# Output projection by pairs of expert chunks for both token tiles of a half batch

## The reference

```python
rw = _gating(hidden_states, sim_matrix, gates)
q = jnp.einsum('bte,bted->btd', rw, jnp.einsum('btc,ecd->bted', hidden_states, q_proj))
...
attn = jnp.einsum('bqk,bkd->bqd', jax.nn.softmax(scores, axis=-1), v)
mixed = attn[:, :, None, :] * rw[..., None]
return jnp.einsum('bted,edc->btc', mixed, o_proj)
```

## Time and profile before

| What | Value |
|---|---|
| time, median of 3 runs | 992.86 us (987.39 to 992.89) |
| the profiled execution | 990.36 us, span 988.6 us |
| mean granted TensorE clock | 0.959 |
| TensorE busy | 924.0 us, 93% of the span |
| VectorE busy | 619.8 us, 63% |
| ScalarE busy | 232.6 us, 24% |
| GpSimd busy | 173.7 us, 18% |
| transfers | 53.68 MB, 54 GB/s over the span |

### The profile page before, as it was taken

One profiled execution on the slowest core, in us unless ns is written; L12 is line 12 of the kernel. 1 busy time (PEld: TensorE's weight loads), 2 busy tenths in 40 slices (PEclk: granted clock), 3 DMA queues, 4 the chain that ended last, 5 costly groups with the idle time before them and its releaser, 6 DMA issues.

```text
span 988.6 us, 15673 instructions
## 1 busy us (share of the span) xinstructions
PE 924.0 (93%) x5000; PEld 844.8 (85%) x5000; DVE 619.8 (63%) x1747; ACT 232.6 (24%) x543; POOL 173.7 (18%) x344
## 2 busy tenths in 40 slices
PE   4787866999999999999999999999999999999987
PEld 3455544999999999998999999999999999999976
DVE  7788773666565656565656575747574657565743
ACT  6666651121111111111111121111111111111111
POOL 4554443530101110101010010101010101001100
PEclk9788886999999999999999999999999999999997
DMA  5454623110202020101010101010101010100010
GB/s 177 150 184 161 213 87 117 65 54 2 64 1 65 1 64 1 65 1 55 10 55 9 54 11 53 11 54 11 53 11 54 11 48 16 48 17 29 26 40 24
DMA packets 30574, 53.68 MB, mean 54 GB/s; under 512 B 7241, under 2 KB 7241, under 8 KB 30386
## 3 DMA queue, kind: packets, MB, share of 16 engines
...
...
## 4 chain that ended last, share of the span: by engine, by line
PE 77%; DVE 4%; issue 2%; DVEq 0%; ACT 0%; POOL 0%; POOLq 0%
PE psQ L1254 51%; PE psO L1341 17%; PE psM L1327 2%; PE psT L1293 2%; PE psT L1229 1%; PE psT L1265 1%; PE psT L1274 1%; PE psQ L1341 1%; DVE acc L1114 1%; PE psM L1311 1%; DVE resid L1144 0%; PE psM L1308 0%; PE psT L1282 0%; DVE neg_mx L1148 0%; DVE b_stats L1059 0%
## 5 line engine op out<-in xcount | busy, mean ns | idle before, releaser
L1254 PE MATMUL psQ<-Wqkv_hi,hT_hi 128*128 128x384 f32 (+1 forms) x1024 | 352.9, 345 | 1.4 <-DVE hT_lo L1055 1.4
L1254 PE MATMUL psQ<-Wqkv_lo,hT_hi 128*128 128x384 f32 (+1 forms) x1024 | 347.3, 339 | 0.0
L1254 PE MATMUL psQ<-Wqkv_hi,hT_lo 128*128 128x384 f32 (+1 forms) x1024 | 347.1, 339 | 0.0
L1114 DVE SCALAR_TENSOR_TENSOR acc<-psQ,RW,acc 128x192 f32<-128x192 f32 x448 | 165.6, 412 | 235.2 <-PE psQ L1254 234.0
L1254 PEld LDWEIGHTS psQ<-Wqkv_hi,hT_hi 128*128 128x128 f32 x1024 | 193.3, 189 | 3.6 <-DVE hT_lo L1055 1.8
L1254 PEld LDWEIGHTS psQ<-Wqkv_lo,hT_hi 128*128 128x128 f32 x1024 | 193.2, 189 | 2.1
L1254 PEld LDWEIGHTS psQ<-Wqkv_hi,hT_lo 128*128 128x128 f32 x1024 | 192.8, 188 | 0.0
L891 POOL TENSOR_TENSOR pow_tmp<-b_mv,eps 128x1 f32<-128x1 f32 x32 | 6.1, 190 | 560.9 <-DVE b_mv L1061 560.8
L1341 PE MATMUL psO<-Wo_hi,mixedT_hi 128*128 128x512 f32 x248 | 98.8, 398 | 0.0
L1341 PE MATMUL psO<-Wo_lo,mixedT_hi 128*128 128x512 f32 x248 | 97.5, 393 | 0.0
L1341 PE MATMUL psO<-Wo_hi,mixedT_lo 128*128 128x512 f32 x248 | 97.4, 393 | 0.0
...
## 6 DMA issues: line engine op xcount, KB each, us to landing
...
```

What stands on the lines that cost most here:

```text
L1114: dve.scalar_tensor_tensor(out=acc[e][:], in0=src, scalar=w, in1=acc[e][:], op0=ALU.mult, op1=ALU.add).then_inc(expert_added, 1)
L1254: last = pe.matmul(psQ[g % 4][:, 0:first_col(g) + PW], x[:, c * P:(c + 1) * P], w[:, c, E + g * PW - first_col(g):E + (g + 1) * PW], start ...
```

## The change

Mixes stay in order, but the second half's mixes are issued one slot later (8 to 11, not 7 to 10), and each mix is followed two slots later by its own part of the projection: two chunks for both tiles of the half, 6 matmuls into `psO` for the even tile and 6 into `psM`, the bank of the scores, for the odd tile. So a half's projection stands in four equal pieces of 12 matmuls, in slots 25 to 28 and 10 to 13; before, it stood in slots 27, 28 and 30 (12, 12 and 24 matmuls) and 11, 12 and 14. The residual additions move from slots 29, 31, 13 and 15 to 28, 29, 13 and 14. Since `psM` is in use until the odd tile's residual addition, the scores of the third tile go from slot 29 to 30 and wait for `y_ready`, and every step behind them in slots 29 to 7 moves one slot on as well: gates, transposes of the probabilities (now slots 0 and 5), q and k of the fourth tile (slot 1), its scores (slot 3), the gates' transposes (6) and the values (7). The semaphore `projected` is replaced by `mix_used` (one step per piece) and `even_projected` (the even tile is complete). SyncE's issues keep their order. The number of instructions that compute is the same on each engine.

```diff
--- before.py
+++ after.py
@@ -34,18 +34,17 @@
 
 
 LEAD = 16
-QK_T_AT = {12: 0, 16: 1, 28: 2, 0: 3}
-SCORES_AT = {16: 0, 18: 1, 29: 2, 2: 3}
-GATES_AT = {17: 0, 19: 1, 30: 2, 3: 3}
-PROBS_T_AT = {18: 0, 20: 1, 31: 2, 4: 3}
-GATES_T_AT = {21: 0, 5: 1}
-VALUES_AT = {22: 0, 6: 1}
+QK_T_AT = {12: 0, 16: 1, 28: 2, 1: 3}
+SCORES_AT = {16: 0, 18: 1, 30: 2, 3: 3}
+GATES_AT = {17: 0, 19: 1, 31: 2, 4: 3}
+PROBS_T_AT = {18: 0, 20: 1, 0: 2, 5: 3}
+GATES_T_AT = {21: 0, 6: 1}
+VALUES_AT = {22: 0, 7: 1}
 MIX_AT = {23: (0, 0), 24: (0, 1), 25: (0, 2), 26: (0, 3),
-          7: (1, 0), 8: (1, 1), 9: (1, 2), 10: (1, 3)}
+          8: (1, 0), 9: (1, 1), 10: (1, 2), 11: (1, 3)}
 MIX_LO_AT = {k + 1: job for k, job in MIX_AT.items()}
-PROJECT_AT = {27: [(0, 0)], 28: [(0, 1)], 30: [(1, 0), (1, 1)],
-              11: [(2, 0)], 12: [(2, 1)], 14: [(3, 0), (3, 1)]}
-Y_AT = {29: 0, 31: 1, 13: 2, 15: 3}
+PROJECT_AT = {k + 2: job for k, job in MIX_AT.items()}
+Y_AT = {28: 0, 29: 1, 13: 2, 14: 3}
 STATS_SLOT, NORM_SLOT, H_T_SLOT = 1, 3, 5
 GATES_1_SLOT, GATES_3_SLOT = 0, 1
 ADD_AT = {0: (), 1: (0, 1), 2: (2,), 3: (3,), 4: (4,), 5: (5,), 6: (6,), 7: (7,)}
@@ -773,7 +772,7 @@
     mix_hi, mix_lo = sem("mix_hi"), sem("mix_lo")
     spread_made = sem("spread_made")
     gatesT_zero = sem("gatesT_zero")
-    projected = sem("projected")
+    mix_used, even_projected = sem("mix_used"), sem("even_projected")
     y_ready = sem("y_ready")
     gate_in_ready, gate_exp_ready = sem("gate_in_ready"), sem("gate_exp_ready")
     rw_ready = sem("rw_ready")
@@ -810,7 +809,7 @@
 
     def tile_copies(k, qkv, lead):
 
-        if k in QK_T_AT and (lead if k == 0 else qkv):
+        if k in QK_T_AT and (lead if k < 2 else qkv):
             return QK_T_AT[k]
         return None
 
@@ -822,10 +821,6 @@
 
         blocks = 2 * (i - i % 2) + 3
         return half[:].rearrange("p (s l) -> p s l", l=P)[:, 1 - i % 2:blocks:2, :]
-
-    def y_bank(i, qkv):
-
-        return psO if qkv or i < TILES - 1 else psQ[0]
 
     def v_twice(i):
 
@@ -857,26 +852,24 @@
                 sp.dma_start(resid[i % 2][:], row(x2_dram, b, i)).then_inc(res_in[i % 2], 16)
 
             def body(b, qkv, lead, prep):
-                for j in range(TILES):
-                    if qkv and (prep or j < TILES - 1):
+                for k in range(SLOTS):
+                    j, g = divmod(k, PAIRS)
+                    if g == 0 and qkv and (prep or j < TILES - 1):
                         sp.wait_ge(h_ready, TILES * b + j + 1)
                         sp.dma_start(X2[:], row(x2_dram, b, j + 1)).then_inc(x2_in, 16)
-                    if not lead and j < 2:
+                    if not lead and g == 0 and j < 2:
                         for n in range(OC // 2):
                             load_wo(j * OC // 2 + n)
-
-                    if lead and j == 0:
+                    if lead and k == 2:
                         load_resid(b - 1, 2)
                         load_resid(b - 1, 3)
-                    if lead and j == 1:
-                        store_y(b - 1, 2)
-                        store_y(b - 1, 3)
-                    if qkv and j == 2:
+                    if lead and k in (14, 15):
+                        store_y(b - 1, k - 12)
+                    if qkv and k == 18:
                         load_resid(b, 0)
                         load_resid(b, 1)
-                    if qkv and j == 3:
-                        store_y(b, 0)
-                        store_y(b, 1)
+                    if qkv and k in (29, 30):
+                        store_y(b, k - 29)
 
             bodies(sp, body, [])
             for p in range(2):
...
@@ -1014,10 +1007,9 @@
                         h, u = MIX_AT[k]
                         act.wait_ge(moved_lo, moves.step())
 
-                        if h == 1:
-                            act.wait_ge(projected, 8 * ab + 3 + u // 2)
-                        elif not isinstance(ab, int) or ab >= 1:
-                            act.wait_ge(projected, 8 * (ab - 1) + 7 + u // 2)
+                        h2 = 2 * ab + h
+                        if not isinstance(h2, int) or h2 >= 1:
+                            act.wait_ge(mix_used, 4 * h2 + u - 3)
                         act.activation(mixedT[0][:, 2 * u:2 * u + 2, :], mixed_f[u % 2][:], ACT.Copy
                                        ).then_inc(mix_hi, 1)
                     if attn and k in SCORES_AT:
@@ -1138,10 +1130,13 @@
 
                     if attn and k in Y_AT:
                         i = Y_AT[k]
-                        a = TILES * ab + i
-                        dve.wait_ge(projected, 2 * a + 2)
-                        dve.wait_ge(res_in[i % 2], 16 * (2 * ab + i // 2 + 1))
-                        dve.tensor_tensor(resid[i % 2][:], y_bank(i, qkv)[:], resid[i % 2][:], ALU.add).then_inc(y_ready, 1)
+                        h2 = 2 * ab + i // 2
+                        if i % 2 == 0:
+                            dve.wait_ge(even_projected, h2 + 1)
+                        else:
+                            dve.wait_ge(mix_used, 4 * h2 + 4)
+                        dve.wait_ge(res_in[i % 2], 16 * (h2 + 1))
+                        dve.tensor_tensor(resid[i % 2][:], (psO, psM)[i % 2][:], resid[i % 2][:], ALU.add).then_inc(y_ready, 1)
                     if attn and k in SCORES_AT:
                         i = SCORES_AT[k]
                         dve.wait_ge(scored, TILES * ab + i + 1)
...
@@ -1298,10 +1293,8 @@
 
                         if i % 2 == 1:
                             pe.wait_ge(exp_done, TILES * ab + i)
-                        elif i == 2:
-                            pe.wait_ge(attT_out, 2 * ab + 1)
-                        elif not isinstance(ab, int) or ab >= 1:
-                            pe.wait_ge(attT_out, 2 * ab)
+                        elif i == 2 or not (isinstance(ab, int) and ab == 0):
+                            pe.wait_ge(y_ready, TILES * ab + i)
                         pe.wait_ge(moved_lo, qk_moved[i])
                         cols = slice(0, (i + 1) * P)
                         q = qkT[:, 0, i * P:(i + 1) * P]
@@ -1328,19 +1321,23 @@
                                              x[:, s * 2 * P:s * 2 * P + cols.stop],
                                              start=(m == 0), stop=(m == len(order) - 1), skip_group_check=True)
                         last.then_inc(valued, 1)
-                    for i, part in PROJECT_AT.get(k, []) if attn else []:
-                        a = TILES * ab + i
-                        bank = y_bank(i, qkv)
-                        if part == 0 and bank is psO and not (isinstance(ab, int) and a == 0):
-                            pe.wait_ge(y_ready, a)
-                        pe.wait_ge(wo_lo, OC)
-                        for c in range(part * HALF, (part + 1) * HALF):
-                            if c % 2 == 0:
-                                pe.wait_ge(mix_lo, 8 * ab + 4 * (i // 2) + c // 2 + 1)
-                            for n, (x, w) in enumerate(products(mixedT, Wo)):
-                                last = pe.matmul(bank[:], x[:, c, place(i)], w[:, c, :],
-                                                 start=(c == 0 and n == 0), stop=(c == OC - 1 and n == 2))
-                        last.then_inc(projected, 1)
+                    if attn and k in PROJECT_AT:
+                        h, u = PROJECT_AT[k]
+                        h2 = 2 * ab + h
+                        if u == 0:
+                            pe.wait_ge(wo_lo, OC)
+                            pe.wait_ge(attT_out, h2 + 1)
+                            if not (isinstance(h2, int) and h2 == 0):
+                                pe.wait_ge(y_ready, 2 * h2 - 1)
+                        pe.wait_ge(mix_lo, 4 * h2 + u + 1)
+                        for i in range(2):
+                            for c in range(2 * u, 2 * u + 2):
+                                for n, (x, w) in enumerate(products(mixedT, Wo)):
+                                    last = pe.matmul((psO, psM)[i][:], x[:, c, place(i)], w[:, c, :],
+                                                     start=(c == 0 and n == 0), stop=(c == OC - 1 and n == 2))
+                            if u == 3 and i == 0:
+                                last.then_inc(even_projected, 1)
+                        last.then_inc(mix_used, 1)
                 if qkv:
                     since_h[0] = moves.k - h_count
```

6 lines of the change are left out of this document (3 added, 3 removed).

## The result

The changed kernel takes 1006.56 us (median of 4 runs, 1004.00 to 1007.29), the kernel before in the same session 992.00 (4 runs, 987.39 to 992.89). The ratio is 1.0156, with a 95% interval of 1.0127 to 1.0186: slower by about 15 us. So the two profiles, 13.6 us apart, can be compared term by term.

A forecast was written before the change was run, and what follows sets the result against it. TensorE's matmuls were taken to bound the kernel, so only its waits could change the time. 990.4 - 4.9 + 14.2 - 0.4 = 999.3 us, plus 5.1 for the clock, gave 1004.4, say 1004 us; range 996 to 1011 for 8 in 10.

The forecast's parts named there:

- one new wait: Slot 10: first projection matmul waits for VectorE's mixedT_lo, 7 times, 1.5 to 2.2 us each in the idle column.
- Part 1: Third and fourth tile one slot on: slot 4's softmax waits in batches 3 to 6 go, -4.9 us.
- Part 2: Projection by pairs: slot 10 waits 2.2 us in batches 2 to 6, 1.6 in 1 and 7, +14.2 us.
- Part 3: Odd tile in the scores' bank: VectorE stands 0.9 us at the even residual, 14 times, at cost 0.
- Part 4: The tail: projection may begin sooner, some 2.8 matmuls issued earlier, -0.4 us.
- Part 5: The clock: three falls to 0.50 in the five long waits, 1.7 us each at least, +5.1 us.
- first rival: The new waits come but the clock stays at 1.00: 999 us, chance 0.25.
- the old wait: Slot 4 of batches 3 to 6: TensorE's transposes (L1265) wait for the softmax; forecast to go.
- rival on the other side: Slot 10: no new wait, VectorE has the low part in time; 985 us, chance 0.10.

The follow-up runs named there:

- written-out loops: Loop over batches 2 to 6 written out, no branch: in the kernel before 985.44 us, in the changed kernel 998.53 us.
- mended kernel: Changed kernel, mix 0's low part ahead of gates_3 and additions in slot 9, fourth tile's q, k transposed in slot 0: 982.93 us; with loop written out 984.49.
- written-out kernel before: The kernel before the change with only the loop over batches 2 to 6 written out: 985.44 us, ratio 0.9950.
- `gate_exp` first: Changed kernel with ScalarE making gate_exp ahead of the rounding of the mix in slots 8 and 24: 993.37 us, ratio 1.0027.
- kernel with the longer wait: Changed kernel with VectorE's row_stats of the next tile ahead of mix 0's low part in slot 9: 1012.33 us; second execution 1015.06 us.

## Why the prediction was right, and where it was off

I had forecast 1004 us (996 to 1011), slower, because of one new wait and its price. It came at that place, for that reason. By the steps:

- **Part 1** (-4.9 us) was mis-sized: it gave -2.6. I had counted the branch from the end of VectorE's last instruction (1.86 us) and so believed that taking 1.1 us of work from ahead of it would move everything behind it. VectorE starts 3.0 to 3.1 us after the queue takes the branch, and only what is not covered of this stands in the idle column. It started no sooner, and q and k's low parts, "just in time" in my words, were 0.6 us late, four times. The written-out loops show that it is the branch; the old slot 0 for the transposes shows that it is this queue.
- **Part 2** (+14.2 us) was right: +15.5. The idle times were 2.15 and 1.52 us where I had 2.2 and 1.6. What I left out is what I had applied in part 1: a matmul's way through the array hides some 0.2 us of each wait in the idle column. The seven waits are 13.8 us there and 15.5 in the slots' lengths, 1.7 more. The difference between batches 2 to 6 and batches 1 and 7 was right as well (forecast 0.6 us, idle times 0.63 apart); its cause is the loop's body.
- **Part 3** (0): right. VectorE stands 1.08 us at the even residual (506.87 in batch 3), nothing behind it is late, and in the mended kernel no slot waits with the two banks in use.
- **Part 4** (-0.4): the last batch and the tail came out 1.4 us longer beyond slot 10's wait. The low stretch there was 3.42 us longer, which no term had. Where both kinds of kernel have 6.83 us of it, the last batch is 128.0 and 128.4 us in the mended kernel (with the loop and without) and 129.7 in the written-out kernel before, so the work may well be shorter, as forecast.
- **Part 5** (+5.1 us, three falls) was mis-sized: one fall of 1.6 us, in each of two profiles. That a fall costs at least half of its stretch, 1.7 us, did not hold in the tail either: 10.24 us less of low clock were 3.1 us (`gate_exp` first). By the Trainium skill's rule ("TensorE: Matmul & The Clock Gate", HAM oscillation) gaps this short cost no clock; the trace disagrees, since a wait of 2.13 us was followed by 3.41 us at 0.50 twice and fourteen longer waits (2.35 to 3.0 us) of the kernel with the longer wait by eight such stretches in two executions. For the change itself the rule was not further off than my three falls: of seven waits six kept the clock. The first rival (999, the clock stays) missed by that one, by the tail's stretch, and by what parts 1 and 2 were off.

So the sum came right in part by luck, because errors cancel: +2.3 for the old wait, +1.3 for the new one and +1.8 in the last batch against -3.5 for the clock in the loop, with -2.0 up to batch 1, which I can't assign to the change. The median (1006.56) lies 2.6 us above the forecast, the profile (1004.00) on it. The rival on the other side (no new wait, 985) is what the kernel becomes when one instruction is moved: 987.5.
